# Attention scores from two fp32r parts of queries and keys, in 64-row tiles of the matrix array

## The reference

```python
w = jnp.einsum('bqhc,bkhc->bhqk', q, k)      # q already scaled; B=4, S=512, NH=16, DH=16
w = jax.nn.softmax(w, axis=-1)
y = jnp.einsum('bhqk,bkhc->bqhc', w, v).reshape(B, S, H)
```

## Time and profile before

| | |
|---|---|
| time, median of 3 runs | 1124.29 us (1120.85 to 1125.54) |
| span of the profiled execution | 1116.0 us |
| what lies around the span, against the median | 8.3 us |
| PE busy | 972.8 us (87%) |
| DVE busy | 655.6 us (59%) |
| ACT busy | 445.6 us (40%) |
| POOL busy | 458.1 us (41%) |
| first to last ST of att0 | 68.5 to 324.8 us |
| first to last ST of att1 | 688.6 to 955.6 us |
| SM and ST matmuls | 512 of each |

### The profile page before, as it was taken

How to read it: one execution, slowest core, us unless ns; L and a number is a source line. 1 busy time by engine, 2 the same in 40 slices (tenths; PEclk the granted TensorE clock), 3 DMA queues, 4 the chain that set the end, 5 groups by cost and what they waited for, 6 DMA issues and landing times.

```text
span 1116.0 us, 13198 instructions
## 1 busy us (share of the span) xinstructions
PE 972.8 (87%) x4652; PEld 500.5 (45%) x4652; DVE 655.6 (59%) x983; ACT 445.6 (40%) x786; POOL 458.1 (41%) x538
## 2 busy tenths in 40 slices
PE   3679999999888858878999998999999998798997
PEld 1232332333237747646655553223333232487852
DVE  3758677677825684675223567775756777246223
ACT  1126656566573213200122213665555665532320
POOL 3333343462526646445222157626355004455420
PEclk8789999999999989989999998999999998999988
DMA  7453333333114300120403235323233320000002
GB/s 236 134 159 113 87 124 97 94 103 97 39 40 159 98 7 1 39 76 30 140 1 123 56 99 147 112 85 105 93 91 115 97 68 32 23 11 1 1 1 75
DMA packets 73665, 89.53 MB, mean 80 GB/s; under 512 B 21080, under 2 KB 56224, under 8 KB 73216
## 3 DMA queue, kind: packets, MB, share of 16 engines
q1 hardware_dynamic: 71264, 86.54, 24.6%
q10 hardware_dynamic: 2336, 2.16, 0.8%
HBM read 64.91 MB, written 23.49 MB: 79 GB/s over the span
## 4 chain that ended last, share of the span: by engine, by line
PE 65%; DVE 14%; SPq 5%; ACT 4%; issue 4%; DMA 4%; POOL 3%; ACTq 0%; DVEq 0%; POOLq 0%
PE PS L540 9%; PE PS L518 8%; PE PS L527 6%; PE PS L989 5%; DVE xnorm L339 5%; PE PS L832 5%; PE PS L974 5%; PE PS L852 5%; PE PS L478 5%; SPq L753 4%; PE PS L488 3%; PE PS L499 3%; PE PS L348 2%; DVE U L690 2%; ACT PH L590 2%
## 5 line engine op out<-in xcount | busy, mean ns | idle before, releaser
L690 DVE TENSOR_REDUCE U<-PS 128x2 f32<-128x1024 f32 x256 | 305.4, 1216 | 93.5 <-PE PS L527 91.2
L590 ACT ACTIVATE PH<-PS 128x512 f32<-128x512 f32 x512 | 280.7, 596 | 148.5 <-PE PS L518 146.6
L518 PE MATMUL PS<-U 98*128 98x512 bf16 x512 | 196.9, 390 | 26.9 <-ACT PH L590 16.7
L527 PE MATMUL PS<-U 96*128 96x512 bf16 x512 | 196.0, 395 | 22.3 <-DVE U L690 12.7
L540 PE MATMUL PS<-PH,U 128*32 128x512 f32 x1024 | 138.5, 613 | 2.3 <-ACT PH L590 1.9
L518 PEld LDWEIGHTS PS<-U 98*128 98x128 bf16 x512 | 49.0, 98 | 196.1 <-ACT PH L590 140.6
L339 DVE TENSOR_SCALAR xnorm<-x,mv,rs 128x256 f32<-128x256 f32 x96 | 86.4, 956 | 68.0 <-POOL rs L331 68.0
L989 PE MATMUL PS<-UR,PHR 128*128 128x256 f32 x512 | 104.3, 286 | 12.0 <-DVE tsc L919 6.7
L1062 POOL TENSOR_TENSOR PHR<-PH,PHR 128x512 fp32r<-128x512 f32 x64 | 85.2, 1338 | 71.7 <-ACT PHR L1026 71.3
L327 POOL TENSOR_TENSOR rs<-ve,mhalf 128x4 f32<-128x4 f32 x24 | 24.4, 1019 | 180.8 <-DVE ve L322 180.3
L989 PEld LDWEIGHTS PS<-UR,PHR 128*128 128x128 f32 x512 | 85.5, 194 | 19.7 <-DVE tsc L919 7.9
(11 more groups left out here) (218 smaller groups left out, 1422.4 us busy)
## 6 DMA issues: line engine op xcount, KB each, us to landing
U<-d_parts SPq DMA_DIRECT2D x384, 64.0 KB, 2.2
d_parts<-U SPq DMA_DIRECT2D x32, 384.0 KB, 2.5
d_o<-U SPq DMA_DIRECT2D x32, 256.0 KB, 2.2
U<-in_L_cond_W_dram SPq DMA_DIRECT2D x8, 1024.0 KB, 9.6
W<-in_L_cond_W_dram SPq DMA_DIRECT2D x6, 1024.0 KB, 6.7
U<-d_o SPq DMA_DIRECT2D x32, 128.0 KB
U<-d_rec SPq DMA_DIRECT2D x16, 256.0 KB
gates<-d_gate SPq DMA_DIRECT2D x3, 1024.0 KB, 5.0
```

The costliest lines, as they stand in the source:

```text
L518: pe.matmul(bank(n % 2), KP[g][0:98, j, kt * P:(kt + 1) * P], QP[g][0:98, j, :], start=True, stop=True).then_inc(self.st_full, 1)
L527: ins = pe.matmul(bank(2 + w % 4), QP[g][0:96, j, qt * P:(qt + 1) * P], KP[g][0:96, j, :], start=True, stop=True)
L590: nc.scalar.activation(PH[:, m % 2, j, :], bank(n % 2), ACT.Exp).then_inc(self.st_read, 1)
L690: v.tensor_reduce(mx[:, G % 2, c:c + 2], PS[:, 2 + (w - 1) % 4:4 + (w - 1) % 4, :], AX.X, ALU.max).then_inc(self.sm_free, 1)
```

## The change

Q and K are split into two fp32r parts each instead of three bf16 parts. Three products (high-high, high-low, low-high) are stacked as 3 x 16 = 48 rows, with the two rows of the maximum 50. Two heads stand above each other: one in rows 0 to 63 of the array, the other in rows 64 to 127. ST of an even step takes the lower half and SM of the same step the upper half; in odd steps it is the other way round. The maximum's columns are put in the new order of heads. A FILL becomes 4 transfers of 48 partitions, WQ and WK 3 transfers each (two of the three slots hold the same part), MROW 4 instead of 2; the constant rows of ones in the key operand are set by 4 small transfers instead of four memsets. The number and the order of TensorE's instructions stay as they are.

```diff
-FILLS = 12 * 16
+FILLS = 4 * 16
+SLOTS = {"Q": (0, 0, 1), "K": (0, 1, 0)}
+SROWS = 48
...
-                        b, g, kt, j = n // 64, n // 16 % 4, n // 4 % 4, n % 4
+                        b, g, kt, r, j = n // 64, n // 16 % 4, n // 4 % 4, 64 * (n % 2), 2 * (n // 16 % 2) + n // 2 % 2
...
-                        pe.matmul(bank(n % 2), KP[g][0:98, j, kt * P:(kt + 1) * P], QP[g][0:98, j, :],
-                                  start=True, stop=True).then_inc(self.st_full, 1)
+                        pe.matmul(bank(n % 2), KP[g // 2][r:r + SROWS + 2, j, kt * P:(kt + 1) * P],
+                                  QP[g // 2][r:r + SROWS + 2, j, :], start=True, stop=True).then_inc(self.st_full, 1)
...
-                        b, g, j, qt = w // 64, w // 16 % 4, w // 4 % 4, w % 4
+                        b, g, r, j, qt = w // 64, w // 16 % 4, 64 - 64 * (w % 2), 2 * (w // 16 % 2) + w // 8 % 2, w // 2 % 4
...
-                        ins = pe.matmul(bank(2 + w % 4), QP[g][0:96, j, qt * P:(qt + 1) * P], KP[g][0:96, j, :],
-                                        start=True, stop=True)
+                        ins = pe.matmul(bank(2 + w % 4), QP[g // 2][r:r + SROWS, j, qt * P:(qt + 1) * P],
+                                        KP[g // 2][r:r + SROWS, j, :], start=True, stop=True)
...
-                    link(eng.tensor_tensor(d[:, 0, :], src, zero, ALU.add))
-                link(eng.tensor_tensor(rest, src, d[:, 0, :], ALU.subtract))
-                link(eng.tensor_tensor(d[:, 1, :], rest, zero, ALU.add))
-                eng.tensor_tensor(d[:, 2, :], rest, d[:, 1, :], ALU.subtract).then_inc(self.split[i], 1)
+                    link(eng.tensor_tensor(d[:, 0, :], src, czero[:, 0:1].to_broadcast([P, T]), ALU.add))
+                eng.tensor_tensor(d[:, 1, :], src, d[:, 0, :].bitcast(F32), ALU.subtract).then_inc(self.split[i], 1)
...
-                        sp.dma_start(d_parts[self.a, 4 * b + 2 * i + k], parts[2 * i + k]).then_inc(self.saved[i], 16)
+                        for slot, c in enumerate(SLOTS[kind[1]]):
+                            sp.dma_start(d_parts[self.a, 4 * b + 2 * i + k, slot].rearrange("d h t -> h d t"),
+                                         parts_d[2 * i + k][:, c, :]).then_inc(self.saved[i], 16)
...
+                        for k, dst in enumerate((QD[g // 2], KD[g // 2])):
+                            src = d_parts[self.a, 4 * b + 2 * (g // 2) + k].rearrange("s d h t -> (s d) h t")
+                            for r in range(2):
+                                sp.dma_start(dst[64 * r:64 * r + SROWS, 2 * (g % 2):2 * (g % 2) + 2, :],
+                                             src[:, 4 * (g % 2) + r:4 * (g % 2) + 4:2, :]).then_inc(self.filled[g], 16)
...
-            att0.set_ones(pool, link)
-            pool.wait_ge(att0.init, 1)
+            att0.set_ones(pool)
```

More of the change, by code:

```diff
@@ L161, in build @@
         rs = sb("rs", [P, 3, TT])
+        ones2 = sb("ones2", [2, T])
         mhalf = sb("mhalf", [P, TT])
@@ L169, in build @@
         H = PH[:, :, :, :].rearrange("p a b t -> p (a b) t")
-        UW = 21504
+        UW = 22112
         UR = alias("UR", [P, UW])
@@ L180, in take, with take_r @@
             return ap if dt == F32 else ap.bitcast(dt)
-        QP = [take(1024, BF16).rearrange("p (j t) -> p j t", j=4) for _ in range(4)]
-        KP = [take(1024, BF16).rearrange("p (j t) -> p j t", j=4) for _ in range(4)]
+        def take_r(words):
+            o = at[0]
+            take(words)
+            return UR[:, o:o + words].bitcast(F32), UR[:, o:o + words]
+        QKU = [[t.rearrange("p (j t) -> p j t", j=4) for t in take_r(2048)] for _ in range(4)]
+        QD, KD = [t[0] for t in QKU[0:2]], [t[0] for t in QKU[2:4]]
+        QP, KP = [t[1] for t in QKU[0:2]], [t[1] for t in QKU[2:4]]
         Vt = take(TT * NH * 32).rearrange("p (k h c) -> p k h c", k=TT, h=NH)
-        parts = [take(768, BF16).rearrange("p (c t) -> p c t", c=3) for _ in range(4)]
+        PTU = [[t.rearrange("p (c t) -> p c t", c=2) for t in take_r(1024)] for _ in range(4)]
+        parts_d, parts = [t[0] for t in PTU], [t[1] for t in PTU]
         q32 = [take(T) for _ in range(4)]
-        resid = take(T)
         Osb = [take(T) for _ in range(2)]
@@ L193, in build @@
         mx = take(32).rearrange("p (a c) -> p a c", a=2)
-        mneg = [take(128, BF16).rearrange("p (i c) -> p i c", i=2) for _ in range(2)]
+        MNU = [[t.rearrange("p (i c) -> p i c", i=2) for t in take_r(256)] for _ in range(2)]
+        mneg_d, mneg = [t[0] for t in MNU], [t[1] for t in MNU]
         rt = [take(T) for _ in range(2)]
@@ L590, in act, with split_part @@
                         nc.scalar.activation(PH[:, m % 2, j, :], bank(n % 2), ACT.Exp).then_inc(self.st_read, 1)
-            def split_part(self, eng, link, kind, b, i, rest):
-                zero = czero[:, 0:1].to_broadcast([P, T])
+            def split_part(self, eng, link, kind, b, i):
                 if b:
-                    eng.wait_ge(self.saved[i], 32 * (self.b0 + b))
+                    eng.wait_ge(self.saved[i], 96 * (self.b0 + b))
                 k = kind == "SK"
@@ L674, in dve_task, with set_ones, set_key_ones @@
                 return task
-            def set_ones(self, eng, link):
-                for g in range(4):
-                    link(eng.memset(KP[g][96:98, :, :], 1.0))
+            def set_ones(self, eng):
                 eng.memset(Vt[:, :, :, HD:2 * HD], 1.0).then_inc(self.init, 1)
+            def set_key_ones(self, sp):
+                for i in range(2):
+                    for r in range(2):
+                        sp.dma_start(KD[i][64 * r + SROWS:64 * r + SROWS + 2, :, :],
+                                     ones2[:, :].unsqueeze(1).to_broadcast([2, 4, T])).then_inc(self.kones, 16)
             def dve(self, v, link):
@@ L758, in task @@
                         for r in range(2):
-                            sp.dma_start(QP[g][96 + r:97 + r, :, :].rearrange("p j (q c) -> p (j q) c", c=P),
-                                         mneg[b % 2][0:16, r, :]).then_inc(self.mset[g], 16)
+                            for c in range(2):
+                                sp.dma_start(QD[g // 2][64 * r + SROWS + c:64 * r + SROWS + c + 1,
+                                                        2 * (g % 2):2 * (g % 2) + 2, :].rearrange(
+                                                            "p j (q c) -> p (j q) c", c=P),
+                                             mneg_d[b % 2][8 - 8 * r:16 - 8 * r, c, :]).then_inc(self.mset[g], 16)
                     elif kind == "OSAVE":
@@ L1367, in setup_dve @@
             link(v.memset(czero[:, :], 0.0))
+            v.memset(ones2[:, :], 1.0)
             v.memset(mhalf[:, :], -0.5).then_inc(consts_set, 1)
@@ L1771, in att1_ones @@
                 v.wait_ge(low_saved, 128)
-                att1.set_ones(v, link)
+                att1.set_ones(v)
             mlp1.dve(v, link, lambda b: cond_norm(v, link) if b == 0 else None,
@@ L1811, in _ @@
                 sp.dma_start(batch(b), A["x"][b].rearrange("(t p) d -> p t d", p=P)).then_inc(ld_x[b], 16)
+            sp.wait_ge(consts_set, 1)
+            att0.set_key_ones(sp)
             save_gates(sp, 0)
@@ L1877, in _ @@
             sp.wait_ge(low_saved, 128)
+            att1.set_key_ones(sp)
             for j in range(4):
```

30 lines of the change are left out of this document (11 added, 19 removed).

## The result

The changed kernel takes 1200.15 us (median of four runs, 1195.28 to 1207.92), the kernel before 1124.26 on the same chip: ratio 1.0697, 95% interval 1.0648 to 1.0746. The forecast was 1114 us. The profiled run took 1197.55 us, its span is 1195.8 us, 79.8 more than the 1116.0 before. The table splits those 79.8 us.

What follows compares the result with a forecast made beforehand. TensorE was taken to bound the kernel, plain groups being a loop through TensorE and ACT. Span 1116.0 + 4.2 - 7.2 - 7.0 = 1106.0, with 8.3 around it 1114 us; range 1090 to 1136, the forecast's own 1106 to 1122.

Steps and rivals of the forecast that it cites:

- TensorE, +4.2: Both attentions: plain groups unchanged, side tasks and groups without SM cost more; +1.8 us in att0, +2.4 in att1.
- The rule on row groups: Streaming groups: a weight load overlaps a matmul only in another row group; would add about 4 us; forecast set it aside.
- the streaming group: Group with a projection between its second and third step, where all score pairs count: 4.26 us forecast against 4.57.
- The first FILL starts about 36.3: Lead of att0: fewer split passes, but twice the bytes of fp32 parts, leave the first FILL's start as before (36.08).
- the lead's -7.2: Lead of att0: shorter SP issues bring the first ST to 61.3 from 68.54, -7.2 us; bounds -3.0 and -8.3.
- The middle, -7.0 from shorter queues: DVE's reciprocal waits for OLOAD behind FILLs, 16.5 us in 6 places; shorter FILLs give -7.0 us, bounds -3 and -16.5.
- SP's queue gives little: Rival: fp32 transfers land later, MROW and OLOAD as late as before; only +4.2 - 3 remain, 1125 us; chance 0.13.
- The clock had 0.07: Rival: the granted clock falls as TensorE streams less, so the gain is gone, 1125 to 1140 us; chance 0.07.
- The 8.3 us around the span: Amount added to the forecast span of 1106.0 us to reach the median, 1114 us.

Runs made afterwards that it cites:

- the repaired form with a busy end: Changed kernel with 128-row saves, each part saved once, plus 26 useless TensorE products per attention where SM has run out: 1116.36 us, ratio 0.9969; run again 0.9986.
- the repeat: The kernel before run again with its instruction order unchanged, against itself: ratio 1.0020.
- the one with the moved loads: The kernel before, with the first MROW and fourth FILL issued ahead of the 13 loads of weights and tables: 1115.52 us, ratio 0.9935.
- the first kernel with 128-row saves: Changed kernel, each save's destination written as 128 rows instead of 8 groups of 16, so scores are of mixed rows: 1130.40 us, ratio 1.0073.
- the changed form with fast saves: Changed kernel with 128-row saves, without useless products: 1130.40 us with rows mixed, 1133.42 unmixed, 1125.46 with each part saved once.

## Why the prediction was wrong

- **TensorE, +4.2: right.** The three prices (0.23 for a pair, 0.11 for the load after a wait, 0.10 for a change of tile) are in the rows. The rule on row groups (the Trainium skill, TensorE: Matmul & The Clock Gate, Part 3) would make the streaming group 4.48, an estimate from that rule and the 0.11; 4.33 was measured, nearer to the 4.26 of the forecast. In the repaired form with a busy end, att0 and att1 take 255.1 and 265.4 us against 256.2 and 267.0, together -2.7; the terms +4.2 and -7.0 say -2.8. That this agrees to 0.1 is luck: the kernel before has 260.1 and 267.0 in its repeat. The steps can be split, though. The six groups of the stalls take 5.9 us less in the repaired form and all other groups 3.2 more; against the other two profiles of the kernel before (the repeat and the one with the moved loads) they take 9.2 and 7.7 less and the others 2.6 and 5.1 more. So both terms have about their size once the saves are fast.
- **"The first FILL starts about 36.3, as before, because twice the bytes of fp32 parts follow each other": the step that failed.** It priced the saves by issue time and bytes and took the rate for that of the kernel before. The diff showed the rearrangement to 8 groups; I read it as a way to order rows, not as the shape on which the rate hangs. It made 42.5 of 36.3, and with the second pair 59.5 of 46, and the lead's -7.2 became +7.7.
- **The rest of the lead: wrong also with fast saves.** In the first kernel with 128-row saves the first ST comes at 66.5, not 61.3, so -2.0 instead of -7.2. Twice the bytes cost time at the full rate too: the third FILL starts at 49.4 where the forecast had 46.3, 4.8 us after its last save was issued. A FILL's transfers are fewer but larger and land later: 192 KB in 4.1 us at the median, where they had 64 KB and 2.2 us. So the first SM comes at 42.66 where the forecast had 40.5 (43.49 before). TensorE's SM were forecast to be ready at 60.2 and are the last thing waited for at 66. Two projections ahead of them take 3.75 and 3.78 us instead of 2.30 and 1.88, the granted clock from 40 to 65 us being 0.61 instead of 0.71; the forecast had no term for this. No run took the lower clock away there, so its cause is open.
- **The middle, -7.0 from shorter queues: wrong sign for the same reason.** The issues did get shorter; the data landed later. With fast saves the reciprocal waits 8 to 13 us in all instead of 52.5; the forecast had next to nothing.
- **The rival "SP's queue gives little" had the place and not the size.** It stopped at gains that do not come (+1.2), where one late load stops DVE, then TensorE, and then halves the clock. Of the 79.8 us of span, shape alone gave back 71.2.
- **The clock had 0.07** on the ground that it stays at 1.00 at att0's end. That row was of the kernel before. In the changed form with fast saves the end often falls to the lower level and loses 5 to 7 us by it. Both kernels have four ST and a PV in such a group, in 2.88 us before and in 3.10 now; whether it is this difference that lowers the clock is not shown, only that more products beside the ST keep it up.
- **"The 8.3 us around the span" was no such thing.** Nearly all runs show 1.8 us between span and time (a few 1.9 to 3.0), so the profiled run of before took about 1117.8 us, 6.5 less than the median. This did not move the forecast, which is the median less 10.0. It does mean that some 4 of the 79.8 us between the two spans are spread between runs: the medians lie 75.9 apart.

## What to carry to other kernels

When a diff rearranges the DRAM side of a transfer, price its outer dimension before its bytes: look at DMA share and GB/s while only such transfers run. A gain of issue time on a queue counts only if the data also land earlier, so follow each late landing through the in-order engines behind it. A stream that is shortened beside a loop that does not need it gives no time, so compare the granted clock of its thin stretches as well.

## What the runs showed of the hardware

- Saves of 256 KB with 2048-byte rows: outer dimension 8, DMA share 0.50 and 184 GB/s; 128 rows, 0.85 and 322 GB/s. The Trainium skill, DMA: Bandwidth & Descriptors, section Why a DMA increments its semaphore by 16 and not by 1, has the rule: a transfer runs on the largest number of engines up to 16 that divides the slowest dimension of both of its patterns, here 8. The shares agree, and the prediction should have weighed it.
- Two fp32r products of 48 and 50 rows in opposite halves mostly start 3 or 4 ns apart and cost one; in the same half SM starts 0.34 after an ST whose load is exposed, and a group with one pair on its path grows by 0.23.
- Products whose result nobody reads made the kernel 0.5 to 0.6% faster (1.0032 to 0.9986 and 0.9969), with the granted clock of 300 to 340 us at 0.93 instead of 0.70.
